# Layer norms of passes 4 and 5: eight scale-and-offset activations on ScalarE in two pieces in place of eight tensor_scalar operations on VectorE

## What is computed

```python
x = _layernorm(x + _L0_gnn_ref(...))   # adj@(f*(adj@(x@W1))), relu, the same again with W2, f2
x = _layernorm(x + _L1_gnn_ref(...))   # concat([x, adj@x]) @ weight
x = _layernorm(x + _L2_gnn_ref(...))   # sigmoid gates from q @ k.T, times adj*adj, @ messages
x = _layernorm(x + _L3_gnn_ref(...))   # silu((adj@x)@W+b), twice
```

## Time and profile before

| | |
|---|---|
| median of three runs | 1653.19 us |
| the profiled execution, its time | 1654.23 us |
| the profiled execution, its span | 1652.4 us |
| TensorE busy | 1605.6 us (97%) |
| VectorE busy | 1212.3 us (73%) |
| ScalarE busy | 1099.3 us (67%) |
| GpSimd busy | 56.0 us (3%) |
| mean granted TensorE clock | 0.995 |

### The profile page before, as it was taken

One profiled execution on the slowest core, in us unless ns is written; L12 is line 12 of the kernel. 1 busy time (PEld: TensorE's weight loads), 2 busy tenths in 40 slices (PEclk: granted clock), 3 DMA queues, 4 the chain that ended last, 5 costly groups with the idle time before them and its releaser, 6 DMA issues.

```text
span 1652.4 us, 19276 instructions
## 1 busy us (share of the span) xinstructions
PE 1605.6 (97%) x7674; PEld 766.8 (46%) x7674; DVE 1212.3 (73%) x1181; ACT 1099.3 (67%) x784; POOL 56.0 (3%) x49
## 2 busy tenths in 40 slices
PE   7999999999999999999999899999999999999997
PEld 4444444444444444444554444444354444444443
DVE  5867547754675568666998698998989986553886
ACT  5767648756778567855666587796878685453753
POOL 2000000000000000000000000100000100000011
PEclk9999999999999999999999999999999999999999
DMA  9988798979699889986888345554545898764983
GB/s 360 416 315 354 283 427 337 369 284 427 269 417 427 333 314 372 411 321 263 355 309 305 140 180 180 178 209 172 199 163 199 312 375 303 282 235 173 351 295 118
DMA packets 67562, 484.56 MB, mean 293 GB/s; under 512 B 7712, under 2 KB 7872, under 8 KB 9232
## 3 DMA queue, kind: packets, MB, share of 16 engines
q1 hardware_dynamic: 66240, 478.70, 75.2%
q0 software_dynamic: 1088, 4.56, 0.8%
q10 hardware_dynamic: 144, 0.07, 0.0%
HBM read 414.09 MB, written 69.21 MB: 292 GB/s over the span
## 4 chain that ended last, share of the span: by engine, by line
PE 81%; DVE 10%; issue 5%; ACT 3%; DMA 1%; POOL 0%; SPq 0%; DVEq 0%; POOLq 0%; ACTq 0%
PE acc L594 34%; PE acc L606 17%; PE spare L594 12%; PE spare L606 6%; PE spare L629 4%; PE rows L498 3%; DVE a_lo L998 3%; DVE a_lo L989 3%; PE acc L629 2%; PE rows L491 1%; DVE bn L905 1%; ACT a_hi L792 1%; DMA a_ring<-adj_dram 1%; DVE gates L1011 1%; ACT gates L822 1%
## 5 line engine op out<-in xcount | busy, mean ns | idle before, releaser
L989 DVE SCALAR_TENSOR_TENSOR a_lo<-a_ring,a_hi 128x2048 f16<-128x2048 f32 x320 | 723.9, 2287 | 321.9 <-ACT a_hi L792 316.5
L792 ACT ACTIVATE a_hi<-a_ring 128x2048 f16<-128x2048 f32 x320 | 604.9, 1905 | 286.7 <-PE spare L594 156.1
L594 PE MATMUL acc<-a_hi,y_hi 128*128 128x512 f16 x1536 | 459.9, 380 | 4.2 <-ACT a_hi L792 3.5
L594 PE MATMUL acc<-a_hi,y_lo 128*128 128x512 f16 x1536 | 459.5, 380 | 0.0
L606 PE MATMUL acc<-a_lo,y_hi 128*128 128x512 f16 x1536 | 406.2, 380 | 9.1 <-DVE a_lo L998 4.9
L606 PEld LDWEIGHTS acc<-a_lo,y_hi 128*128 128x128 f16 x1536 | 149.7, 98 | 193.5 <-DVE a_lo L998 8.1
L594 PEld LDWEIGHTS acc<-a_hi,y_lo 128*128 128x128 f16 x1536 | 150.7, 98 | 182.3 <-issue 2.2
L594 PEld LDWEIGHTS acc<-a_hi,y_hi 128*128 128x128 f16 x1536 | 150.5, 98 | 182.0 <-issue 6.0
L1011 DVE SCALAR_TENSOR_TENSOR gates<-gates,a_ring 128x1024 f32<-128x1024 f32 x128 | 155.8, 1218 | 35.8 <-ACT gates L822 35.6
L805 ACT ACTIVATE a_hi<-gates 128x1024 f16<-128x1024 f32 x128 | 134.8, 1053 | 41.2 <-DVE gates L1011 41.0
L998 DVE TENSOR_TENSOR a_lo<-gates,a_hi 128x1024 f16<-128x1024 f32 x128 | 155.5, 1215 | 0.0
(11 more groups left out here) (119 smaller groups left out, 760.9 us busy)
## 6 DMA issues: line engine op xcount, KB each, us to landing
a_ring<-adj_dram SPq DMA_DIRECT2D x326, 1024.0 KB, 7.4
saved_squares<-squares SPq DMA_DIRECT2D x64, 1024.0 KB, 12.6
a_ring<-saved_squares SPq DMA_DIRECT2D x64, 1024.0 KB, 4.8
x_T<-xt_dram SPq DMA_DIRECT2D x4, 512.0 KB, 8.6
x_rows<-x_dram POOLq DMA_DIRECT2D x1, 2048.0 KB, 12.9
out_dram<-x_rows POOLq DMA_DIRECT2D x3, 512.0 KB, 2.9
out_dram<-x_rows SPq DMA_DIRECT2D x2, 256.0 KB, 2.0
w<-W_dram POOLq DMA_DIRECT2D x2, 64.0 KB, 5.4
```

The costliest lines, as they stand in the source:

```text
L594: mm = pe.matmul(sums[:, h * BANK:(h + 1) * BANK], blk(y[:, y_pass % 2, :], st.j0 + s), slot(a_hi, st)[:, s, h * BANK:(h + 1) * BANK], sta ...
L792: act.activation(slot(a_hi, st), loaded(st), ACT.Copy, scale=2.0 ** A_EXP).then_inc(s_ahi, 1)
L989: dve.scalar_tensor_tensor(out=slot(a_lo, st).rearrange("p s c -> p (s c)"), in0=loaded(st).rearrange("p s c -> p (s c)"), scalar=2.0 ** A ...
```

## The change

The norms of passes 4 and 5 leave VectorE. `normalise` is taken out of their stages. `shift` is added on VectorE one offset after `ln_moments`, and `normalise_again` on ScalarE in two pieces of four blocks each, at offsets 4 and 5 (pass 4) or 5 and 6 (pass 5). In pass 5 everything that follows the norm moves by one offset, on all three engines, and the epilogue's length goes from 11 to 12. `values` gets a wait for the norm of the chunk before, `root` on GpSimd as well. By the table the epilogue of (5,1) starts at unit 296 instead of 295, and that of (5,2) at 308 instead of 306; (5,3) stays at 320.

```diff
--- before.py
+++ after.py
@@ -70,6 +70,7 @@
     "nonlin": {6: 1, 7: 1, 8: 1},
     "resid": {6: 1, 8: 1},
     "root": {4: 1, 5: 1, 6: 2, 8: 1},
+    "shift": {4: 1, 5: 1, 6: 1},
     "ln": {4: 1, 5: 1, 6: 1, 8: 1},
     "msg": {5: 1},
     "qk": {5: 2},
@@ -175,7 +176,7 @@
 
 
 LAST_GATED = 10 + GATED
-LENGTH = {0: 1, 1: 4, 2: 3, 3: 4, 4: 8, 5: 11, 6: 23, 7: 4, 8: 10, LAST_GATED: 14}
+LENGTH = {0: 1, 1: 4, 2: 3, 3: 4, 4: 8, 5: 12, 6: 23, 7: 4, 8: 10, LAST_GATED: 14}
 
 
 def timing(p, k):
@@ -570,7 +571,7 @@
                 2: {2: [project]},
                 3: {2: [project]},
                 4: {2: [project], 8: [x_transposes]},
-                5: {2: [project], 6: [x_transposes], 7: [messages], 8: [queries], 10: [message_rows]},
+                5: {2: [project], 7: [x_transposes], 8: [messages], 9: [queries], 11: [message_rows]},
                 6: {3: [project]},
                 7: {1: [project]},
                 8: {3: [project]},
@@ -754,7 +755,7 @@
 
             def normalise_again(blocks):
                 def go(p, k):
-                    act.wait_ge(s_shift, k + 1)
+                    act.wait_ge(s_shift, nth("shift", p, k))
                     for b in blocks:
                         op = act.activation(x_chunk(p, k)[:, b, :], val[:, b, :], ACT.Identity,
                                             bias=stats[:, 2, b:b + 1], scale=stats[:, 1, b:b + 1])
@@ -771,9 +772,11 @@
                 1: {0: [evacuate], 1: [save_w_qk], 2: [y_high]},
                 2: {0: [evacuate, relu_z], 2: [y_high]},
                 3: {0: [evacuate], 3: [y_high]},
-                4: {0: [evacuate], 6: [y_high], 8: [save_x_T]},
-                5: {0: [evacuate], 6: [save_x_T], 7: [save_m_T], 8: [qk_high(0, kT_hi, K_EXP)],
-                    9: [qk_high(1, qT_hi, Q_EXP)], 10: [y_high]},
+                4: {0: [evacuate], 4: [normalise_again(range(HB))], 5: [normalise_again(range(HB, CB))], 6: [y_high],
+                    8: [save_x_T]},
+                5: {0: [evacuate], 5: [normalise_again(range(HB))], 6: [normalise_again(range(HB, CB))],
+                    7: [save_x_T], 8: [save_m_T], 9: [qk_high(0, kT_hi, K_EXP)], 10: [qk_high(1, qT_hi, Q_EXP)],
+                    11: [y_high]},
                 6: {1: [evacuate], 5: [relu], 20: [normalise_again(range(HB))], 21: [normalise_again(range(HB, CB))],
                     23: [y_high]},
                 7: {0: [evacuate], 2: [silu], 3: [y_high]},
@@ -866,6 +869,7 @@
                     right, op = over_features((f1c if p == 1 else f2c)[:, i * CB:(i + 1) * CB]), ALU.mult
                 else:
                     right, op = x_chunk(p, k), ALU.add
+                    dve.wait_ge(s_ln, nth("ln", p, k) - 1)
                 dve.tensor_tensor(val[:, :, :], rows[:, :, :], right, op).then_inc(s_val, 1)
 
             def split_bias(src, dst, done):
@@ -952,7 +956,7 @@
 
             def shift(p, k):
 
-                dve.wait_ge(s_root, nth("root", p, k, 1))
+                dve.wait_ge(s_root, nth("root", p, k, PER_CHUNK["root"][p] - 1))
                 dve.scalar_tensor_tensor(out=stats[:, 2, :], in0=moments[:, :, 0], scalar=-1.0, in1=stats[:, 1, :],
                                          op0=ALU.mult, op1=ALU.mult).then_inc(s_shift, 1)
 
@@ -971,9 +975,9 @@
                 1: {0: [take_over], 1: [values], 2: [y_low]},
                 2: {0: [take_over], 2: [y_low, split_biases]},
                 3: {0: [take_over], 2: [values], 3: [y_low]},
-                4: {0: [take_over], 2: [values, ln_moments(0, s_val, "val"), normalise], 6: [y_low]},
-                5: {0: [take_over], 2: [values], 3: [ln_moments(0, s_val, "val"), normalise],
-                    8: [qk_low(0, kT_hi, kT_lo, K_EXP)], 9: [qk_low(1, qT_hi, qT_lo, Q_EXP)], 10: [y_low, add_beta]},
+                4: {0: [take_over], 2: [values, ln_moments(0, s_val, "val")], 3: [shift], 6: [y_low]},
+                5: {0: [take_over], 2: [values], 3: [ln_moments(0, s_val, "val")], 4: [shift],
+                    9: [qk_low(0, kT_hi, kT_lo, K_EXP)], 10: [qk_low(1, qT_hi, qT_lo, Q_EXP)], 11: [y_low, add_beta]},
                 6: {8: [ln_moments(0, s_nl, "nonlin")], 10: [times_gamma], 13: [affine_residual],
                     16: [ln_moments(1, s_res, "resid")], 19: [shift], 23: [y_low]},
                 7: {3: [y_low]},
@@ -1053,6 +1057,8 @@
 
             def root(run):
                 def go(p, k):
+                    if p < GATED and (p, k) != (4, 0):
+                        pool.wait_ge(s_ln, nth("ln", p, k) - 1)
                     if p > GATED or (p == GATED and (run or k)):
                         pool.wait_ge(s_ln, NC * (p - 4) + k if p == GATED else NC * 3)
                     root_of(range(CB), nth("root", p, k, run))
```

## The result

| | median us | range, runs |
|---|---|---|
| before | 1653.22 | 1652.88 to 1655.44, 4 |
| after | 1664.43 | 1663.02 to 1664.86, 4 |

The ratio is 1.0063 [1.0048, 1.0078]: the change makes the kernel slower by some 11 us. The profiled execution took 1664.41 us with a span of 1662.6, against 1654.23 and 1652.4 before. Lines moved a little: after the change `root` is L1055, `shift` L960, `normalise_again` L760, `a_lo` L993, `take_over` (`z_T`) L852, the epsilon add L915, a sigmoid L825.

What follows compares the result with a forecast made beforehand. TensorE, busy 1605.6 of 1652.4 us, was taken as the bound, so only its waits could be won (ceiling 10.0 us). The terms 2.1 + 1.7 - 2.2 + 0.4 + 6.3 + 1.1 - 2.8 gave +6.6: 1659.8 us, range 1654.5 to 1665.

Steps and rivals of the forecast that it cites:

- as summed: Whole kernel: the forecast's own sum of terms holds, 1657.5 to 1662.5 us; chance 0.55.
- The root beside `a_lo`: All eight epilogues: root takes 3.57 us instead of 1.67, `shift` ends its wait at T + 3.94 (T: epsilon add's start).
- Rival A: Passes 4 and 5: root not held up by `a_lo`, stays 1.67 us; 1650 to 1652 us; chance 0.08.
- (4,0), +2.1 and half clock: Pass 4, chunk 0: `z_T` and transposes 2.1 us later, TensorE idle about 3.0 us, then half clock costing 1.7.
- (4,2), -2.2: Pass 4, chunk 2: the `a_lo` TensorE waited for ends before it is due, winning 2.2 us.
- (4,3), +0.4: Pass 4, chunk 3: a 0.6 us wait is won, yet the next pass starts 0.4 us later.
- (5,0) to (5,2), 2.1 each: Pass 5, chunks 0 to 2: TensorE waits 2.1 us each for the norm on ScalarE, +6.3 in all.
- End of pass 5, +1.1: Entry of the gates: `y_high` and `message_rows` of (5,2) now precede sigmoid 2; -0.7, +2.3 and -0.5 us.
- (5,3), -2.8: Pass 5, chunk 3: low half's wait of 2.4 us and half clock of 1.7 won, 1.35 lost before logit 10.
- the term for the clock: TensorE's waits: clock falls after 2.25 us idle, not after 2.12; so half clock, +1.7 us, counted at (4,0).
- Rival B: Passes 4 and 5: clock falls behind two to four new waits, 1.7 us each; 1663 to 1667 us; chance 0.17.

Runs made afterwards that it cites:

- after once more: The changed kernel again, unchanged, beside other follow-up kernels: 1662.74 us, ratio 1.0061 to the kernel before.
- pass 4 alone: The change without its edits of pass 5, so only pass 4's norm goes to ScalarE: 1654.07 us, ratio 1.0005 to the kernel before.
- one piece: The changed kernel with pass 5's two norm pieces on ScalarE joined in one at offset 5: 1660.00 us, ratio 1.0041 to the kernel before.
- pass 5 alone: The change without its edits of pass 4, so only pass 5's norm goes to ScalarE: 1663.64 us, ratio 1.0057 to the kernel before.
- the norm late in pass 4: The kernel before with pass 4's norm still on VectorE but one offset later: 1650.63 us, ratio 0.9980 to the kernel before.

## Why the prediction was right, and where it was short

The predicted 1659.8 us lay 4.6 below the measured 1664.4. That is inside the range of 1654.5 to 1665, but near its top and above the 1657.5 to 1662.5 that "as summed" meant; slower had the chance of 0.80. Some luck is in it, for the profiled execution at least: it took 3.2 us less ahead of the changed passes, which no term had, and without that it would have lain above the range. By its own steps:

- **The root beside `a_lo`.** Taken at 3.57 us from pass 8; in passes 4 and 5 it was 3.55 to 3.58, and 2.48 at (5,3). `shift` came at T + 3.90 and T + 3.94, forecast T + 3.94. Rival A falls, and no run has its own case, a short root beside a working VectorE. The run with the shift ahead of the `a_lo` comes nearest (short root, but VectorE idle meanwhile), at a ratio of 1.0004.
- **(4,0), +2.1 and half clock.** Counted from T, the transposes came 2.08 us later (649.52 - 627.73 = 21.79, before 650.68 - 630.97 = 19.71). The wait was 2.70 us where 3.0 was forecast. The fall of the clock came in this execution and stayed away in three others with the same wait of 2.70 us: after once more, pass 4 alone, and one piece.
- **(4,2), -2.2.** The wait is gone in the view of waits. **(4,3), +0.4:** the milestones give +0.35.
- **(5,0) to (5,2), 2.1 each.** Each was 2.08 us, of which the view of waits shows 1.92. This is the largest term, and pass 5 alone carries nearly the whole loss (1.0057 of 1.0063).
- **End of pass 5, +1.1**, and **(5,3), -2.8:** both as summed. The parts of the first were -0.7, +2.1 and -0.3 by TensorE's waits, where -0.7, +2.3 and -0.5 were forecast. At (5,3) the wait is 1.17 us where 1.35 was forecast. Its -1.7 for half clock held between these two profiles, but the same low half's wait (2.32 and 2.26 us) left the clock whole in the profiles of pass 4 alone and of the norm late in pass 4, so it too was no sure gain.
- **What was short** is the term for the clock: "After 2.25 us of idling the clock fell, after 2.12 and 2.06 it did not. I therefore count the half clock here". It took one execution for a boundary. In the profile of after the clock fell behind waits of 1.92, 1.92 and 2.12 us, and behind one of 2.00 at 1343 us where the same wait in the profile of before was followed by a clock of 1.00. So the term is no count of waits above a length; each wait of some 2 us and more has a chance of costing 1.7 us. Over the thirteen profiles of this document, waits of 2.12 us before a sigmoid come 22 times, and the clock fell behind 10 of them; behind the 2.70 us for `z_T` it fell once in four, behind the 1.92 us for the normalised rows twice in nine. Rival B had this, with its condition ("just below the 2.25") and its price (1663 to 1667 us), and the profiled execution is its case. Over the nine runs of the changed kernel, it lay between 1660.8 and 1665.5.

Without any term for the clock the forecast's sum is also +6.6, as its +1.7 at (4,0) and -1.7 at (5,3) cancel. The rest that the runs show at full clock is +7.2 to +7.4. What is missing is thus mostly half clock: +2.0 us in the mean of the five later runs, whose loss was 9.4 us, and +5.1 between the two profiled executions (5.1 in passes 4 and 5, 1.7 in pass 6, less 1.7 at the start), of which the unexplained 1.5 us at the start take some back.

Open: in which of the unprofiled runs the clock fell at which wait (only its mean is listed for these), and why one execution loses it behind a wait and the next does not.

## What to carry to other kernels

Before a step is taken off an engine, look at what it waits for: here VectorE's cost was the wait for the root, and putting the norm behind the next low half took that away without moving the norm, while on ScalarE the norm of pass 5 was ready 5.0 us later (T + 9.09 against T + 4.07), by the drawn-out root and by what stood in ScalarE's queue. Before, it ended on VectorE at 805.82 + 2.14 = 807.96, with T = 803.89:

```profile
805.82 2.14 DVE L924 TENSOR_SCALAR x_rows<-val,moments,stats 128x128 f32<-128x128 f32 x8 [1.75 <-POOL stats L1051]
```

An operation that is 1.6 us by itself must be priced beside the neighbour that the change gives it. And where one engine is bound throughout, count each new wait of about 2 us with a possible fall of the clock, not only with its length.

## What the runs showed of the hardware

- GpSimd's root on 128x8 values took 1.64 to 1.67 us with VectorE idle, 3.55 to 3.62 beside a `scalar_tensor_tensor` of 2.29 us that started before it, and 2.48 to 2.55 beside one of 1.22 that a second operation of 1.22 followed at once. The Trainium skill (SBUF — State Buffer, section "Who interferes with whom") says that a VectorE instruction with two inputs in SBUF, as the `a_lo` has them, keeps GpSimd from reading SBUF. By that rule the root could do its work only when the `a_lo` has ended: in (5,0) at 802.62 + 2.29 = 804.91, ended by 804.91 + 1.64 = 806.55. The trace agrees, with 806.41.
- The same wait in the same kernel lets the granted clock fall to 0.50 in one execution and not in another: 2.70 us behind `z_T` (0.50 in one profile of after, whole in the second and in those of pass 4 alone and of one piece), 1.92 us in pass 5 (0.50 behind two of three, then behind none in the second profile and in that of pass 5 alone). The Trainium skill (TensorE: Matmul & The Clock Gate, section "Part 1: The HAM clock gate (the "warmup" mystery)") says that the monitor runs freely and isn't reset when a kernel starts, so that the count of slow matmuls differs between runs of one kernel. It says so of a kernel's start. The traces here show executions that differ in this way in the middle of a kernel; they do not show that its reason is theirs.
